# Each block's norm in the tail of the block before it, biases first, output by tile, and two orders inside blocks

## The reference

```python
def _layernorm(x, axis=-1, eps=1e-05):
    m = jnp.mean(x, axis=axis, keepdims=True)
    v = jnp.var(x, axis=axis, keepdims=True)
    return (x - m) / jnp.sqrt(v + eps)

    x = x + _L0_attn_ref(_layernorm(x), ...)             # retention, gated feed-forward inside
    x = x + _L0_xattn_ref(ctx_1024, _layernorm(x), ...)  # selective state space
    x = x + _L0_ffn_ref(_layernorm(x), ...)              # ternary weights
    x = x + _L1_attn_ref(_layernorm(x), ...)             # multi-query attention, biases
    x = x + _L1_xattn_ref(_layernorm(x), fside, ctx)     # smooth-quantised linears
    x = x + _L1_ffn_ref(_layernorm(x), ...)              # 16 experts, 2 per token
    x = x + _L2_attn_ref(_layernorm(x), ...)             # causal attention, biases
    x = x + _L2_xattn_ref(_layernorm(x), ctx_1024, ...)  # attention to two contexts
    x = x + _L2_ffn_ref(_layernorm(x), ...)              # BitLinear: ternary weights, two norms
    x = x + _L3_attn_ref(_layernorm(x), ...)             # column softmax attention
    x = x + _L3_xattn_ref(_layernorm(x), ctx_1024, ...)  # cross attention
    x = x + _L3_ffn_ref(_layernorm(x), ...)              # 4 experts, 1 per token
```

```python
            def step(state, xs):
                d_t, B_t, C_t, u_t = xs
                dA = jnp.exp(d_t[..., None] * A)
                state = state * dA + (d_t * u_t)[..., None] * B_t[:, None, :]
                y_t = jnp.einsum('ben,bn->be', state, C_t)
                return (state, y_t)
```

## Time and profile before

| what | value |
| --- | --- |
| median of 3 runs | 2459.95 us (2458.89 to 2461.53) |
| the profiled execution | 2458.84 us |
| its span | 2457.0 us |
| mean granted TensorE clock | 0.876 |
| PE, DVE, ACT, POOL busy | 1913.7, 1313.9, 748.0, 298.2 us |
| instructions | 25650 |
| read from and written to device memory | 72.97 and 11.27 MB |

### The profile page before, as it was taken

The page is one execution under the profiler, slowest core; times in us unless marked ns, Lnnn a source line. Parts: engine busy times, 40 slices in busy tenths (PEclk is TensorE's granted clock), DMA queues, the critical chain, the costliest instruction groups (busy, mean ns, idle before and its releaser), DMA issues.

```text
span 2457.0 us, 25650 instructions
## 1 busy us (share of the span) xinstructions
PE 1913.7 (78%) x9024; PEld 1225.1 (50%) x9024; DVE 1313.9 (53%) x3103; ACT 748.0 (30%) x1773; POOL 298.2 (12%) x267
## 2 busy tenths in 40 slices
PE   6674656978448399999757825799999799998696
PEld 3431223645434156666545513555555477777353
DVE  6648788654862344444586576433333566665122
ACT  4224234204121033333421401133333355554010
POOL 3510000000112200000120132100000222220101
PEclk9886777999758799999866957899999999998798
DMA  3010000000441200000000020200000200003101
GB/s 134 1 52 0 0 0 18 1 27 1 175 174 64 84 28 1 1 1 1 35 0 1 21 118 0 117 3 1 1 1 1 104 1 1 1 1 116 44 22 44
DMA packets 21901, 85.73 MB, mean 35 GB/s; under 512 B 2834, under 2 KB 15900, under 8 KB 17680
## 3 DMA queue, kind: packets, MB, share of 16 engines
q1 hardware_dynamic: 19472, 77.96, 8.2%
q0 software_dynamic: 2304, 6.15, 0.8%
HBM read 72.97 MB, written 11.27 MB: 34 GB/s over the span
## 4 chain that ended last, share of the span: by engine, by line
PE 65%; DVE 17%; issue 7%; POOL 4%; DMA 3%; ACT 2%; SPq 1%; POOLq 1%; DVEq 0%; ACTq 0%
PE bank L136 53%; PE bank L141 7%; PE bank L3210 3%; PE bank L3232 2%; DMA space<-expert_rows 1%; DVE space L2808 1%; DVE space L178 1%; SPq L1873 1%; DVE space L783 1%; DVE space L788 1%; POOLq L3678 1%; DVE space L1341 1%; DVE space L774 1%; DMA space<-in_L_attn 1%; POOL space L623 1%
## 5 line engine op out<-in xcount | busy, mean ns | idle before, releaser
L136 PE MATMUL bank<-space 128*128 128x256 f32 (+14 forms) x6706 | 1471.9, 430 | 199.6 <-DVE space L783 77.8
L136 PEld LDWEIGHTS bank<-space 128*128 128x128 f32 (+8 forms) x6706 | 899.8, 184 | 708.9 <-issue 372.0
L141 PE MATMUL bank<-consts,space 128*128 128x128 f32 (+1 forms) x1610 | 261.1, 307 | 295.1 <-DVE space L189 79.6
L141 PEld LDWEIGHTS bank<-consts,space 128*128 128x128 f32 (+1 forms) x1610 | 205.3, 156 | 369.2 <-issue 166.7
L197 POOL TENSOR_TENSOR space<-space,consts 128x4 f32<-128x4 f32 x26 | 29.4, 1131 | 678.7 <-DVE space L184 678.7
L136 PE MATMUL bank<-space,consts 128*128 128x512 f32 (+2 forms) x148 | 94.8, 803 | 7.0 <-DVE space L2962 5.8
L2498 POOL TENSOR_TENSOR space<-space,consts 128x4 f32<-128x4 f32 x64 | 68.5, 1071 | 218.2 <-DVE space L2429 218.2
L2247 DVE TENSOR_REDUCE space<-bank 128x2 f32<-128x512 f32 x64 | 44.1, 689 | 86.8 <-PE bank L136 86.7
L2293 ACT ACTIVATE space<-bank,space 128x256 f32<-128x256 f32 x128 | 59.4, 469 | 95.7 <-DVE space L2247 95.7
L3210 PE MATMUL bank<-space 128*128 x176 | 82.0, 611 | 3.1 <-DVE space L3326 3.1
L233 ACT ACTIVATE space<-bank 128x512 f32<-128x512 f32 x28 | 16.6, 596 | 222.9 <-PE bank L141 222.9
(11 more groups left out here) (326 smaller groups left out, 2017.0 us busy)
## 6 DMA issues: line engine op xcount, KB each, us to landing
space<-in_L_ffn SPq DMA_DIRECT2D x13, 2048.0 KB, 11.8
space<-in_L_attn SPq DMA_DIRECT2D x10, 2048.0 KB, 13.5
space<-in_L_xattn SPq DMA_DIRECT2D x4, 2048.0 KB, 9.7
expert_rows<-space SPq DMA_DIRECT2D x16, 128.0 KB, 7.3
space<-expert_rows SPq DMA_DIRECT2D x16, 128.0 KB, 2.2
expert_results<-space SPq DMA_DIRECT2D x16, 128.0 KB, 1.7
space<-in_L_xattn SPq DMA_DIRECT2D x1, 1919.0 KB, 19.5
space<-in_L_xattn SPq DMA_DIRECT2D x1, 1536.0 KB, 6.4
```

The source lines that it names most:

```text
L136: return self.nc.tensor.matmul(out, lhsT, rhs, start=first, stop=last, skip_group_check=True)
L141: return self.nc.tensor.transpose(out, src, eye)
```

## The change

- A shared buffer `c.normed` and shared `c.norm_stats` hold every block's norm (`SPACE` shrinks by 2128). `Stage.final` runs in the DVE code of the block before: tile i's `bn_stats` after the x add of tile i+1 is issued, the moments after tiles 3 and 7, and all eight normalisations behind the last tile. POOL computes the powers at the end of its code for that block, before its drain. The first block's norm stays at its start.
- In Causal, Column and Cross tiles are added in pairs, those of the first half in mid-block; statistics and first moments come there.
- Output biases are added to x by POOL at the block's start, once its weights have landed; DVE's add waits for it. Retention adds `hs` to x in two DVE instructions of 128x1024 within its up loop, and POOL's adds are gone.
- The output is stored by tile as TopExpert's sums end.
- StateSpace's sums lag two units. The C row of n is spread at even t, the B row of n + 1 at odd t, each behind a sum.
- Ternary turns a quarter between the gate and the up matmuls of the unit, and ACT's copy is one unit later.
- SmoothQuant has its own buffer for rows, and Experts gathers into `xT`'s space, since `c.normed` is taken.

```diff
+    def final(self, e, i, ready):
+        norm = self.ahead
+        if norm is None:
+            return
+        e.wait_ge(*ready(i + 1))
+        norm.stat(e, i)
+        if i % 4 == 3:
+            norm.moments(e, i // 4)
+        if i == NT - 1:
+            norm.normalise(e, 0)
+            norm.normalise(e, 1)
...
+    def stat(self, e, i):
+        c = self.c
+        c.nc.vector.bn_stats(self.stats[:, i, :], self.src[:, i, :]).then_inc(*c.v.next())
+
+    def moments(self, e, g):
+        c, nc = self.c, self.c.nc
+        e.wait_ge(*c.v.so_far)
+        for i in range(4 * g, 4 * g + 4):
+            nc.vector.bn_aggr(self.mv[:, i, :], self.stats[:, i, :]).then_inc(*c.v.next())
+        e.wait_ge(*c.v.so_far)
+        cols_ = slice(4 * g, 4 * g + 4)
+        nc.vector.tensor_scalar(self.rs[:, 1, cols_], self.mv[:, cols_, 1], 1.0, self.eps,
+                                ALU.mult, ALU.add).then_inc(*self.s.var.one)
+
+    def normalise(self, e, g):
+        e.wait_ge(*self.s.inverse(g + 1))
+        for i in range(4 * g, 4 * g + 4):
+            self.c.nc.vector.tensor_scalar(self.out[:, i, :], self.src[:, i, :], self.mv[:, i, 0:1],
+                                           self.rs[:, 0, i:i + 1], ALU.subtract, ALU.mult).then_inc(*self.s.normed.one)
...
 class Retention(Stage):
-        self.norm.vector(e)
...
+            if p in (1, 4):
+                ts = slice(p // 4 * 4, p // 4 * 4 + 4)
+                e.wait_ge(*s.scaled2.all)
+                nc.vector.tensor_tensor(c.x[:, ts, :], c.x[:, ts, :], self.hs[:, ts, :], ALU.add).then_inc(*s2.x_h.one)
+        for i in range(NT):
+            e.wait_ge(*s2.down_mm(i + 1))
+            e.wait_ge(*s2.x_h(i // 4 + 1))
+            nc.vector.tensor_tensor(c.x[:, i, :], c.x[:, i, :], bk[4 + i % 4][:, 0:D], ALU.add).then_inc(*s2.h_done.one)
+            if i:
+                self.final(e, i - 1, s2.h_done)
+        self.final(e, NT - 1, s2.h_done)
...
 class StateSpace(Stage):
-        for t in range(N + 4):
-            if t >= 4:
-                u = t - 4
+        for t in range(N + 2):
+            if t >= 2:
+                u = t - 2
                 n, f = self.UNITS[u]
                 e.wait_ge(*s.weighted(u + 1))
                 for g in range(NG):
                     done = c.mm(bk[2 * f + g], c.ident, self.db[u % 4][:, cut(g)], n == 0, n == SSM_N - 1)
                 done.then_inc(*s.summed.one)
+            if t == 0:
+                self.spread_row(e, 0, 0)
             if t < N and t % 2 == 0:
...
+                self.spread_row(e, t // 2, 1)
+            if t + 1 < N and t % 2 == 1:
+                self.spread_row(e, t // 2 + 1, 0)
...
+    def spread_row(self, e, n, j):
+        c, s, bk = self.c, self.s, self.c.banks
+        if j == 0 and n:
+            e.wait_ge(*s.spread_out(2 * n))
+        if j == 1 and n:
+            e.wait_ge(*s.weighted(2 * n))
+        for g in range(NG):
+            if n == 0 and j == 0:
+                e.wait_ge(*s.split(g + 1))
+            c.mm(bk[4 + 2 * j + g], self.select[0:self.R0, SSM_N * j + n, :],
+                 self.parts[0:self.R0, g * HALF:(g + 1) * HALF]).then_inc(*(s.c_spread if j else s.b_spread).one)
...
 class Ternary(Stage):
-            if f % 2 == 1 and g == 1 and f + 1 < self.FT:
-                self.turn_quarter(e, f // 2 + 1)
             for up, counted in enumerate((s.gate_mm, s.up_mm)):
+                if up and u % 4 == 3 and f + 1 < self.FT:
+                    self.turn_quarter(e, f // 2 + 1)
...
-            if at == 2 and n + 1 < self.QUARTERS:
+            if at == 3 and n + 1 < self.QUARTERS:
                 self.quarter_out(e, n + 1)
...
 class Projection:
-    def vector(self, e):
+    def vector(self, e, final):
         c, s = self.c, self.s
         for i in range(NT):
             e.wait_ge(*s.out_mm(i + 1))
+            e.wait_ge(*s.biased(i + 1))
             c.nc.vector.tensor_tensor(c.x[:, i, :], c.x[:, i, :], self.banks[i % 4][:, 0:D],
                                       ALU.add).then_inc(*s.added.one)
+            if i:
+                final(e, i - 1, s.added)
+        final(e, NT - 1, s.added)
...
 class Heads(Stage):
+        if "bo" in self.w:
+            e.wait_ge(*s.biased(n // TPB + 1))
         done = c.nc.vector.tensor_tensor(
...
+        for i in (n, n + 1):
+            self.final(e, i, lambda m: s.added((m + 1) // TPB))
 
     def add_bias(self, e):
         c, s = self.c, self.s
+        e.wait_ge(*self.ld.all)
+        e.wait_ge(*self.norm.s.normed.all)
         for m in range(4):
-            e.wait_ge(*s.added(m + 1))
             x = c.x[:, TPB * m:TPB * (m + 1), :]
-            c.nc.gpsimd.tensor_tensor(x, x, repeat(self.w["bo"], TPB), ALU.add)
+            c.nc.gpsimd.tensor_tensor(x, x, repeat(self.w["bo"], TPB), ALU.add).then_inc(*s.biased.one)
...
                 stage.gpsimd(e)
+                if stage.ahead is not None:
+                    stage.ahead.gpsimd(e)
                 e.drain().then_inc(*c.over.one)
...
-            e.wait_ge(*c.over(4 * (last - first)))
+            finished = stages[-1][1].finished
             for i in range(NT):
+                e.wait_ge(*(c.over(4 * (last - first)) if finished is None else finished(i + 1)))
                 e.dma_start(od[:, i, :], c.x[:, i, :]).then_inc(*stored.one)
```

More of the change, by code:

```diff
@@ L177, in vector @@
                     e.wait_ge(*ready(i + 1))
[L178 to L190, removed]
+                self.stat(e, i)
+            self.moments(e, g)
+        for g in (0, 1):
+            self.normalise(e, g)
+    def stat(self, e, i):
[15 more added lines that the diff above has]
+                                           self.rs[:, 0, i:i + 1], ALU.subtract, ALU.mult).then_inc(*self.s.normed.one)
     def gpsimd(self, e):
@@ L245 @@
 class Stage:
+    ahead = finished = None
+    def final(self, e, i, ready):
[9 more added lines that the diff above has]
+            norm.normalise(e, 1)
     def tensor(self, e):
@@ L291, in __init__ @@
         self.c, self.w, self.ld = c, w, ld
-        self.hs = c.sb(NT, D)
-        self.norm = Norm(c, self.hs, c.x)
+        self.hs = c.normed
+        self.norm = c.norm
         self.r, self.junk = c.sb(3, NT), c.sb(D)
@@ L665, in __init__ @@
         self.c, self.w, self.ld = c, w, ld
[L666 to L667 removed]
+        self.z = c.normed
+        self.norm = c.norm
         self.pads, self.u = c.bufs(3, HALF // S, 3 + S), c.sb(DC, TOK)
@@ L708, in tensor @@
                 done.then_inc(*s.summed.one)
+            if t == 0:
+                self.spread_row(e, 0, 0)
             if t < N and t % 2 == 0:
[L710 to L720, removed]
-                             self.parts[0:R0, cut(g)]).then_inc(*s.spread_mm.one)
+                self.spread_row(e, t // 2, 1)
+            if t + 1 < N and t % 2 == 1:
+                self.spread_row(e, t // 2 + 1, 0)
         for i in range(NT):
@@ L1158, in gpsimd @@
         for i in range(NT):
-            e.wait_ge(*s.added(i + 1))
-            c.nc.gpsimd.tensor_tensor(c.x[:, i, :], c.x[:, i, :], self.bias, ALU.add)
+            c.nc.gpsimd.tensor_tensor(c.x[:, i, :], c.x[:, i, :], self.bias, ALU.add).then_inc(*s.biased.one)
 class MultiQuery(Stage):
@@ L1586, in vector @@
         self.down.vector(e, lambda e, b: e.wait_ge(*s.a_ready(b + 1)))
+        for i in range(NT):
+            self.final(e, i, lambda n: s.added((n + 1) // TPB))
     def scalar(self, e):
@@ L1896, in __init__ @@
         self.xT = c.sb(DC, TOK)
-        mark = [list(p) for p in c.pools]
-        xn = c.sb(NT, D)
-        self.norm = Norm(c, xn, c.x)
-        self.turned = Turned(c, self.xT, xn, c.banks[0:4])
-        c.pools = mark
+        self.norm = c.norm
+        self.turned = Turned(c, self.xT, c.normed, c.banks[0:4])
     def tensor(self, e):
@@ L2900, in gpsimd @@
         c, s, t, nc = self.c, self.s, self.t, self.c.nc
-        self.norm.gpsimd(e)
+        e.wait_ge(*self.ld.all)
+        e.wait_ge(*self.norm.s.normed.all)
+        self.out.gpsimd(e)
         nc.gpsimd.memset(self.kd.rearrange("p a b c -> p (a b c)"), 0.0).then_inc(*s.kd_clear.one)
@@ L3634, in program @@
             c.stage, c.used, c.dmas, c.late_ready = n, 0, 0, late_loaded
+            c.norm = Norm(c, c.normed, c.x, room=c.norm_stats)
             stages.append((n, BLOCKS[n][2](c, views, loaded)))
+        for (_, stage), (_, following) in zip(stages, stages[1:]):
+            stage.ahead = following.norm
         stored = Signal(c.semaphore("stored"), 0, NT, 16)
@@ L3662, in _ @@
                 begun(e, n)
+                if n == first:
+                    stage.norm.vector(e)
                 stage.vector(e)
```

122 lines of the change are left out of this document (58 added, 64 removed).

## The result

The changed kernel takes 2427.39 us (median of 3 runs, 2426.01 to 2428.01) against 2459.95. The ratio is 0.9866, with a 95% interval of 0.9844 to 0.9888: 1.3% faster. The forecast was 2428, from 2411 to 2446. The profiled execution took 2427.39 us, its span is 2425.6.

What follows compares the result with a forecast made beforehand. Each block has its own limit; StateSpace's loop was bound by DVE's chain plus its wait for PE's sums. Terms summed to -31.7 us from the profiled 2458.84: 2427.1, or 2428 against the median, range 2411 to 2446.

Steps and rivals of the forecast that it cites:

- The loop: StateSpace's loop: DVE stops waiting for sums, 9.04 us a pair instead of 11.29; 33.7 us, taken as -31.
- Into StateSpace: Barrier into StateSpace: PE's matmuls open the block, so the norm in the tail before it costs +3.2 us.
- Into Ternary: Barrier into Ternary: dense DVE tail adds 2.9 us, ACT's passes now start with the barrier; +1.5 us.
- Into Experts: Barrier into Experts: zero fills that POOL's scatters wait for start later with the barrier; +4.4 us.
- Into Cross: Barrier into Cross: +4.4 us for the norm ahead of context matmuls, +2 for PE's lower clock; together +6.4.
- Into TopExpert: Barrier from Cross into TopExpert: usual gain from the norm in the tail, small memsets staying; -1.5 us.
- Into Causal: Barrier from Experts into Causal: statistics fit between POOL's late gathers; -2.3 us.
- the norm moves nearly cancel: All barriers and mid-block statistics: gains and losses of moving the norm put at +1.6 us together.
- The first rival: Barriers into Experts, Cross and StateSpace: 12 to 14 us of losses vanish in slack; about 2415 us, chance 0.13.
- the second: StateSpace's loop: PE or ACT becomes the limit, gaining 16 us rather than 31; about 2443 us, chance 0.20.
- fourth: StateSpace's loop: the wait stays because another signal held DVE, loop gain 0; about 2459 us, chance 0.05.
- the third: StateSpace's loop: the B row behind a sum replaces the wait, 3 us a pair; about 2470 us, chance 0.04.

Runs made afterwards that it cites:

- store_only: The kernel before with only the output stored tile by tile; 2457.9 us in a single run.
- lag_only: The kernel before with StateSpace's sums lagging two units, both rows of a pair still spread at even steps; 2455.78 us in a single run.
- rows_only: The kernel before with the next pair's B row spread at odd steps, sums still four units behind; 2456.23 us in a single run.
- warm: The changed kernel with 40 unused matmuls added at the end of TensorE's program in Retention and Column; 2436.59 us.
- warm18: The changed kernel with 18 unused matmuls added at the end of TensorE's program in Retention and Column; 2421.5 us, ratio 0.9843.
- norm_only: The changed kernel with the old orders in StateSpace and Ternary and the output stored after the last barrier; 2472.41 us, ratio 1.0048.

## Why the prediction was right

The time was right to 0.6 us, which is more than its terms deserve: their misses have both signs. The mechanism of the loop, which carries the gain, was right.

*The loop* was the gain, as forecast, by the mechanism forecast: DVE's chain of 4.52 us a step became the limit, 9.04 a pair, and PE and ACT kept up. The size was 33.7 (173.92 from first to last scan before, 140.23 after), the full arithmetic; the 2.7 us that I took off for handoffs were not needed. The clock helped: PE at 0.84 rather than 0.73 over the loop had more room than I had counted.

*Into StateSpace* the term of +3.2 was too small; it measures +8.4 with 2.9 of it booked under Ternary. From the last add to the first scan it is 36.92 before and 42.40 after, +5.5, and 4.0 of it are the barrier. PE now starts at the lower clock, 2.6 us slower over its first matmuls; I had applied that to Cross alone, though PE had idled only 1.37 ahead of L136 here too. But that this makes the other 1.5 isn't shown: three kernels with the old code up to there and these matmuls at 3.70 (store_only, lag_only, rows_only) read 39.0 and not 36.92 there, and from PE's start to the first scan warm, with the matmuls at 3.67, took 38.9, the changed kernel 38.3, warm18 36.8. The other 2.9, of the dense tail, were right (13.86 to 16.73 from the last scan's start to the last add).

*Into Ternary* +1.5 less 2.9 leaves -1.4 for this block by my own count; measured is nothing (100.18 and 100.14).

*Into Experts* +4.4 became +9.0. The barrier is +4.7 and POOL's scatter +5.3 late, as I said. Then PE, which had done the shared expert's work meanwhile, idled 16.05 us and not 7.12 before the first rows; from there to SP's issue of the first result it was 18.4 and not 16.1, at a granted clock of 0.68 and not 0.79. The rest, 1.5, is spread. In warm18, with the same norm, the same stretch took 15.7 at 0.81, so this part depends on where the clock happens to rise.

*Into Cross* +6.4 was right in both halves: 4.2 for the barrier, 3.0 for the clock, where I had put 2.

*Into TopExpert* -1.5 became +0.5. PE did start 1.56 earlier, as forecast, but the step failed that ends there: the zero fills came 4.1 later with the barrier and became what POOL's scatter waits for, 27.65 us after the last add and not 26.38. I named no cost for them here, though I had at Experts.

*Into Causal* the barrier came 5.14 after the last add, not 4.1, released by POOL's queue; the sign was right.

*The sum of the norm's terms* in the prediction is +5.6 where its text says +1.6; the total of -31.7 was added up rightly. Measured alone, the moves cost 12.9. So "the norm moves nearly cancel" was wrong by 7 against the sum and by 11 against the 1.6; the largest misses are Experts (4.6) and the way into StateSpace. The loop (2.7), Ternary's order (4.2 of waits removed and not 3) and the scatter of single blocks made up for it: that the total came out to 0.6 us is luck. The range has a slip as well: -10 and +18 around 2428 would be 2418 to 2446, and 2411 was written.

The output's term was right (3.3, measured 3.6). The first rival (hidden barrier losses) is refuted by norm_only, the second and fourth by the loop; the third by the changed kernel, while lag_only shows that it lay close.

## What to carry to other kernels

Moving a step ahead of a barrier pays only where that step was what the next block waited for; elsewhere it moves the barrier and every transfer, fill and matmul tied to it. Read block by block what ends the first wait: here putting six of eleven norms back took 25 us off. Of the five left in the tail MultiQuery, SmoothQuant, Causal and BitLinear were shorter by 2.4 to 4.5 us in the changed kernel than before, and Column shows no gain (+1.1). And price a pause of TensorE by what follows it: 5.5 us of idling made the run of 32 matmul records behind it 42% longer, and a few matmuls without a use, placed in the pause, took that back.

## What the runs showed of the hardware

After 4.6 to 5.5 us without work TensorE's next matmuls started at the lower of its two levels: the 32 of Cross took 0.32 us each on average rather than 0.22 (10.20 and 7.17 in all), the 16 transposes behind them 1.91 as before; with 4.18 us of added matmuls in the pause and 0.56 to 1.47 us of idling left, Cross's 32 took 7.17 again. The blocks whose code was the same differ by up to 5 us between traces (MultiQuery 129.6 to 134.6), so a single block in a single trace says little below that.
